# New hand-planned step orders for all five engines of an attention kernel

## The chip, the cores and the metric

The kernel runs on one core of one Trainium2 chip. A core has TensorE (PE) for matmuls, VectorE (DVE), ScalarE (ACT) and GpSimd (POOL) for elementwise work, and SyncE (SP), whose queue here issues every DMA. The metric is the device time in microseconds (us) of one execution; the median of several runs is compared.

## The reference

A layer of conditioned attention with a residual, over 8 batches of 512 rows and 1024 columns, 16 heads of 64, all in float32:

```
scale, shift = split(cond @ W_emb + b_emb)
xn  = rms_norm(x, g_norm) * (1 + scale) + shift
q, k, v = heads(xn @ W_qkv);  q, k = rms_norm(q, g_q), rms_norm(k, g_k)
o   = softmax(q k^T / 8) v                 # per head
out = x + o + o @ W_out
```

## The kernel before

Every float32 operand of a matmul is split into a high and a low part (names ending in `_hi`, `_lo`; `q_split` and `v_split` hold both), and a product is made of two or three matmuls. For every split ACT makes the high part and DVE or POOL subtracts it to get the low part.

Work comes in batches (8) and pairs of heads (8 in a batch, so 4 couples of two pairs). The projection to q, k, v of a couple of pairs uses seven products in place of eight, on sums of blocks of xn and of the weights. The weights are split once, in batch 0: loaded raw into `w_raw` and its like, summed (DVE takes even blocks, POOL odd ones), split into a ring `w_ring` of 15 chunks, and stored to `qkv_store` and `wo_store`. Later batches reload them from there, each unit as soon as the ring's space is free. So batch 0 has much more DVE, ACT, POOL and DMA work than the others. Before it comes a short stage that computes scale and shift.

The order of work on each engine is written out by hand, as a table of steps in three versions: `HEAD` for batch 0, `BODY` for batches 1 to 6, `TAIL` for batch 7. A step is a pair number, a letter and a number: `0C8` is step 8 of kind C for pair 0, in BODY pairs 8 to 11 are the next batch's 0 to 3, and a + in place of the pair means work for the next batch. The same letter on two engines means two parts of the same thing. Each engine runs its list strictly in order, and steps wait for each other through semaphores. The letters used below:

- PE: `C` a part of a tile of the projection (six matmuls, lines 597 to 599), `P` the same of the output projection, `T` turning q and k, `S` scores, `F` turning probabilities into `flip_bank` (two banks), `W` product with v (line 732), `X` turning x, `Z` turning scale and shift.
- ACT: `A` sum of squares of a tile of x (line 769), `X` modulation, `Y` high part `xa_hi` of an operand, `E` copy of a projection tile, `S` exponential, `F` `pt_hi`, `O` half of o, `Q` `o_hi`, `V`, `D`, `L` (high part of a weight unit).
- DVE: `G` a sum of blocks of xn (line 1007), `Y` low part `xa_lo` (line 1058), `J` a sum of weight blocks, `L` low part of the even half of a weight unit (line 908), `D` line 1089, `S` `neg_max`, `N` scaling of `probs` by the row sums (line 1075), `F` `pt_lo` (line 1079), `R` adding the residual.
- POOL: `X` low part `xa_lo` (line 1178) of half of the operands, `J` and `L` the odd halves, `A` and `D` the reciprocal roots, `M`, `V`, `Q` (`o_lo`).
- SP: `W` reload of a weight unit (line 1266), `H` store of one (line 1254), `G` raw weights (line 1241), `X` a tile of x for the next batch (line 1275), `E` a tile of x for the residual (line 1300), `O` store of output (line 1309).

An example of a step's waits, the residual load on SP in batch 0, which wants every qkv weight unit split because it lands in `w_raw`:

```
if is_first(b) and g < NFIRST:
    for done in w_lo_even, w_lo_odd:
        sp.wait_ge(done, PAIRS // 2 * COUPLE)
```

And the product with v on PE waits for `pt_lo` of the same step, since that frees its `flip_bank`: `freed(pe, "F", n, it)`.

Of the kernel before, what the change touches and what calls it, by code (L numbers as in the profile page):

```python
# [40 lines left out]
        1F7 2C21 1W6 1W7 2C22 2C23 2C24 2T0 2T1 2C25 2C26 2C27 4C0 4C1 2S0 2S1 4C2 2S2 2S3 4C3 2S4 2S5 2S6 2S7 3T0 4C4
        3T1 2F0 4C5 4C6 2F1 2W0 2F2 4C7 3S0 3S1 2F3 2W1 2W2 3S2 2F4 4C8 3S3 4C9 4C10 2W3 2W4 2F5 3S4 3S5 2F6 4C11 2F7
        2W5 2W6 2W7 3F0 3F1 3S6 3S7 3F2 3W0 3W1 4C12 4C13 4C14 3F3 4C15 4C16 4C17 3W2 3W3 4C18 3F4 3F5 4C19 4C20 3W4 3W5
        4C21 3F6 3F7 4C22 4C23 4C24 4C25 3W6 3W7 4C26 4C27 4T0 4T1 6C0 6C1 6C2 6C3 +X0 +X4 4S0 4S1 +X1 +X5 6C4 6C5 4S2
        4S3 +X2 +X3 4S4 4S5 6C6 +X6 4F0 6C7 4S6 4S7 4W0 4F1 4F2 5T0 5T1 6C8 6C9 4W1 4W2 6C10 4F3 +X7 6C11 5S0 5S1 4F4
# [25 lines left out]
        L1 8T0 L2 7O1 8T1 9D1 7Q0 9D2 8V1 L3 8S0 8S1 9D3 8S2 8S3 L4 L5 L6 8F0 8S4 8F1 8S5 L7 8F2 8S6 8S7 9T0 8F3 9T1 8F4
        8O0 8F5 9S0 9S1 8F6 8F7 9S2 9S3 9F0 9V0 9S4 9S5 9S6 9F1 10E0 10E1 9V1 9F2 9S7 8O1 10E2 10D0 9F3 9F4 9F5 10E3
        10D1 9F6 9F7 10D2 L8 10D3 11D0 L9 L10 L11 11D1 10T0 10V0 10V1 10T1 11D2 10S0 11D3 10S1 L12 L13 L14 10S2 10S3
        10S4 L15 10F0 10S5 10S6 10S7 10F1 11T0 11T1 11S0 11S1 11S2 11S3 8Q0 9O0 12E0 9O1 10F2 10F3 9Q0 12E1""".split(),
    "VectorE": """
        X0 X4 Y0 0J0 X2 0J1 0J2 Y1 Y4 G0 G1 G2 G3 X6 G4 G5 Y5 0D0 0L4 G6 0J3 0L5 0L6 Y3 Y2 0J4 G7 0L7 0D1 0E4 0E5 0J5
        0L8 0E6 0L9 0L10 0L11 0E7 0E8 0E9 0D2 Y6 0D3 0E10 0L12 0L13 1D0 0E11 1D1 2L0 2L1 0E12 0T0 0T1 0E13 0S0 0S1 2L2
        0N0 2L3 1D2 0S2 0S3 1D3 0N1 0N2 0N3 0S4 0S5 0F0 0F1 0N4 0N5 0S6 0S7 0F2 0F3 0N6 0N7 2J0 2J1 1T0 0F4 0O0 0F5 1T1
        2J2 2J3 0F6 1S0 0F7 2D0 2L4 2L5 1S1 1N0 2L6 2L7 1N1 1S2 1S3 2E4 0O1 2D1 2L8 2E5 1S4 1S5 1N2 1N3 2L9 2J4 2E6 1S6
        1S7 1F0 2E7 1F1 1N4 1N5 1N6 1N7 1F2 1F3 2E8 2J5 2L10 1F4 2D2 2E9 1F5 2L11 2D3 1F6 1F7 2E10 2L12 2L13 1O0 1O1  # L80
        2E11 3D0 3D1 4L0 4L1 2T0 2E12 2E13 2T1 3D2 3D3 2S0 2S1 4L2 4L3 2N0 2S2 2S3 2S4 2S5 2S6 2S7 4J0 2N1 4J1 4J2 2N2
        2N3 2N4 3T0 2F0 2N5 2N6 4J3 4L4 3T1 +A0 +A1 +A2 2N7 2F1 2F2 3S0 +A3 4L5 3S1 3S2 2F3 4D0 2F4 3S3 3N0 3N1 4L6 4L7
# [1310 lines left out]
```

## Time and profile before

| what | us |
|---|---|
| median of 3 runs (lowest, highest) | 2259.87 (2258.46, 2263.42) |
| span of the profiled execution | 2255.9 |
| PE, DVE, ACT, POOL busy in it | 2176.2, 1748.6, 1411.7, 931.4 |

The profiled execution's span lies 4.0 us below the median of the timed runs. In the profile a matmul's duration includes its way through the array, and matmuls overlap; the distance from one start to the next is what one costs. A bracket at a row's end gives the idle time of the engine just ahead of that instruction, and who ended it. Busy time by stretch is printed as start:end, length, then for each engine the busy time and the count of instructions in brackets, then the granted TensorE clock as a share of 2.4 GHz (0.50 is the lower level, 1.2 GHz), the share of DMA time and GB/s.

### The profile page before, as it was taken

To read this page: it belongs to the slowest core of one execution; us is meant where nothing else is said; L and a number is where in the kernel's file an instruction comes from. 1 tells how busy PE (TensorE), PEld (TensorE's weight loads), DVE (VectorE), ACT (ScalarE), POOL (GpSimd) and SP (SyncE) were. 2 spreads that over 40 slices of the span, in tenths; PEclk is the share of its full clock that TensorE was granted. 3 is DMA by queue.
4 is the path that set the end of the run, shared out by engine and by line. 5 is a ranking of instruction groups with operands and counts; after the bars stand their busy time and mean duration, and the time that the engine had idled before them with its cause. 6 is when DMAs were issued, how large, how long until landed. Compare 5 with 4: busy or idle time off the path is not lost.

```text
span 2255.9 us, 39472 instructions
## 1 busy us (share of the span) xinstructions
PE 2176.2 (96%) x13392; PEld 1992.2 (88%) x13392; DVE 1748.6 (78%) x3511; ACT 1411.7 (63%) x3077; POOL 931.4 (41%) x1241
## 2 busy tenths in 40 slices
PE   7788789999999999999999999999999999999999
PEld 3676678999999999999999999999999999999989
DVE  4799988678985699767986689857897569876786
ACT  4577766467854577546864578646775458754663
POOL 3866674235532345223541246312553325422330
PEclk9899999999999999999999999999999999999999
DMA  7655464777556765568555675566654775656842
GB/s 299 238 212 226 188 224 147 269 269 254 192 187 241 271 218 196 175 236 289 207 202 197 230 285 192 189 238 242 230 205 165 254 281 199 203 192 227 294 157 103
DMA packets 141528, 497.55 MB, mean 221 GB/s; under 512 B 14864, under 2 KB 61968, under 8 KB 140304
## 3 DMA queue, kind: packets, MB, share of 16 engines
q1 hardware_dynamic: 141328, 495.03, 61.7%
q8 instruction: 108, 1.77, 0.3%
q14 instruction: 92, 0.75, 0.1%
HBM read 425.77 MB, written 69.21 MB: 219 GB/s over the span
## 4 chain that ended last, share of the span: by engine, by line
PE 77%; DVE 11%; issue 4%; DMA 4%; ACT 3%; POOL 1%; SPq 0%; DVEq 0%; ACTq 0%
PE proj_bank L597 16%; PE proj_bank L599 16%; PE proj_bank L598 16%; PE flip_bank L721 8%; PE pv_bank L732 5%; PE pv_bank L733 5%; PE score_bank L713 4%; PE score_bank L714 4%; DMA w_ring<-qkv_store 2%; DVE neg_max L1069 2%; DVE probs L1075 2%; PE score_bank L686 2%; DVE pt_lo L1079 1%; ACT pt_hi L866 1%; ACT probs L860 1%
## 5 line engine op out<-in xcount | busy, mean ns | idle before, releaser
L597 PE MATMUL proj_bank<-w_ring,xa_hi 128*128 128x384 f32 x1792 | 626.5, 350 | 21.0 <-DVE xa_lo L1058 7.6
L599 PE MATMUL proj_bank<-w_ring,xa_lo 128*128 128x384 f32 x1792 | 606.4, 338 | 0.0
L598 PE MATMUL proj_bank<-w_ring,xa_hi 128*128 128x384 f32 x1792 | 605.7, 338 | 0.0
L860 ACT ACTIVATE probs<-score_bank,neg_max 128x512 f32<-128x512 f32 x512 | 352.1, 690 | 250.0 <-DVE neg_max L1069 242.6
L866 ACT CAST pt_hi<-flip_bank 128x512 fp32r<-128x512 f32 x512 | 296.3, 586 | 235.7 <-PE flip_bank L721 148.3
L1079 DVE TENSOR_TENSOR pt_lo<-flip_bank,pt_hi 128x512 fp32r<-128x512 f32 x512 | 346.6, 686 | 117.0 <-ACT pt_hi L866 111.6
L1069 DVE TENSOR_REDUCE neg_max<-score_bank 128x1 f32<-128x512 f32 x512 | 341.4, 684 | 75.0 <-PE score_bank L714 71.7
L597 PEld LDWEIGHTS proj_bank<-w_ring,xa_hi 128*128 128x128 f32 x1792 | 340.6, 190 | 40.8 <-issue 13.5
L598 PEld LDWEIGHTS proj_bank<-w_ring,xa_hi 128*128 128x128 f32 x1792 | 341.3, 190 | 9.6
L599 PEld LDWEIGHTS proj_bank<-w_ring,xa_lo 128*128 128x128 f32 x1792 | 339.6, 190 | 0.0
L721 PE MATMUL flip_bank<-ident,probs 128*128 128x128 f32 x2048 | 294.3, 274 | 14.5 <-DVE probs L1075 7.3
L721 PEld LDWEIGHTS flip_bank<-ident,probs 128*128 128x128 f32 x2048 | 245.9, 141 | 59.4 <-issue 12.5
L1075 DVE TENSOR_SCALAR probs<-probs,row_inv 128x512 f32<-128x512 f32 x512 | 277.9, 543 | 18.2
L597 PE MATMUL proj_bank<-w_ring,o_hi 128*128 128x256 f32 x992 | 285.4, 288 | 0.0
L599 PE MATMUL proj_bank<-w_ring,o_lo 128*128 128x256 f32 x992 | 280.3, 283 | 0.0
L598 PE MATMUL proj_bank<-w_ring,o_hi 128*128 128x256 f32 x992 | 279.8, 282 | 0.0
L1190 POOL TENSOR_TENSOR qk_rstd<-qk_ms_eps,neg_half 128x4 f32<-128x4 f32 x256 | 269.1, 1051 | 20.0
L1171 POOL TENSOR_TENSOR v_split<-stage,v_split 128x256 fp32r<-128x256 f32 x128 | 97.0, 758 | 431.1 <-ACT v_split L833 430.6
L732 PE MATMUL pv_bank<-pt_hi,v_split 128*128 128x512 f32 x512 | 219.9, 430 | 14.1 <-DVE pt_lo L1079 13.5
L713 PE MATMUL score_bank<-k_hi,q_split 128*128 128x512 f32 x512 | 214.0, 418 | 14.2 <-ACT probs L860 8.3
L1187 POOL TENSOR_TENSOR qk_ms_eps<-qk_ms,eps_col 128x4 f32<-128x4 f32 x256 | 62.0, 242 | 393.7 <-DVE qk_ms L1089 393.6
L967 DVE TENSOR_TENSOR stage<-proj_bank,stage 128x384 f32<-128x384 f32 x256 | 141.2, 555 | 105.2 <-PE proj_bank L599 101.4
(91 smaller groups left out, 3855.3 us busy)
## 6 DMA issues: line engine op xcount, KB each, us to landing
w_ring<-qkv_store SPq DMA_DIRECT2D x392, 768.0 KB, 5.7
w_ring<-wo_store SPq DMA_DIRECT2D x108, 512.0 KB, 4.7
qkv_store<-w_ring SPq DMA_DIRECT2D x56, 768.0 KB, 4.9
x_tile<-in_x SPq DMA_DIRECT2D x36, 512.0 KB, 7.8
w_raw<-in_x SPq DMA_DIRECT2D x112, 128.0 KB, 6.4
out<-w_raw SPq DMA_DIRECT2D x112, 128.0 KB, 1.9
w_raw<-in_w_qkv SPq DMA_DIRECT2D x16, 768.0 KB, 7.8
wo_store<-w_ring SPq DMA_DIRECT2D x16, 512.0 KB, 5.0
```

The lines of the kernel that those rows point to most:

```text
L597: nc.tensor.matmul(dst, a_hi, w[:, 0, :], start=start, stop=False, skip_group_check=shared)
L598: nc.tensor.matmul(dst, a_hi, w[:, 1, :], start=False, stop=False, skip_group_check=shared)
L599: return nc.tensor.matmul(dst, a_lo, w[:, 0, :], start=False, stop=stop, skip_group_check=shared)
L713: nc.tensor.matmul(score_bank[n % 2][:, :], q_t, k_hi[h][:, :], start=True, stop=False)
L721: mm = nc.tensor.transpose(flip_bank[u % 2][:, qt * P:(qt + 1) * P], probs[h][:, qt, i * P:(i + 1) * P], ident[:, :])
L732: nc.tensor.matmul(pv_bank[h][:, :], v_t, pt_hi[n % 2][:, :], start=(i == 0), stop=False)
L860: nc.scalar.activation(probs[h][:, i, :], score_bank[n % 2][:, :], ACT.Exp, bias=neg_max[:, n:n + 1], accum_out=row_sum[:, n:n + 1]).then_ ...
L866: nc.scalar.copy(pt_hi[n % 2][:, :], flip_bank[u % 2][:, :]).then_inc(flip_hi, 1)
L1069: nc.vector.tensor_reduce(neg_max[:, n:n + 1], score_bank[n % 2][:, :], AX.X, ALU.max, negate=True).then_inc(max_done, 1)
L1075: nc.vector.tensor_scalar(probs[h][:, i, :], probs[h][:, i, :], row_inv[:, n:n + 1], None, ALU.mult).then_inc(probs_ready, 1)
L1079: nc.vector.tensor_tensor(pt_lo[n % 2][:, :], flip_bank[u % 2][:, :], f32(pt_hi[n % 2][:, :]), ALU.subtract).then_inc(flip_freed["VectorE" ...
L1190: nc.gpsimd.tensor_tensor(qk_rstd[:, n, :], qk_ms_eps[:, n, :], neg_half[:, :], ALU.pow).then_inc(qk_rstd_done, 1)
```

## The change

Only the three tables are replaced. Each engine's list in each table holds exactly the same steps as before, in another order; no step moves to another engine, and the code that carries them out is the same (13 lines lower, since the tables are longer). Steps shift by 1 to 3 places on average, at most 34, and on SP in BODY by 8 on average, at most 47. The new orders were planned with DVE's two-tensor operations taken as longer while POOL runs. Two lines of the 311 stand for the rest, the start of DVE's list in HEAD:

```diff
-        X0 X4 Y0 0J0 X2 0J1 0J2 Y1 Y4 G0 G1 G2 G3 X6 G4 G5 Y5 0D0 0L4 G6 0J3 0L5 0L6 Y3 Y2 0J4 G7 0L7 0D1 0E4 0E5 0J5
...
+        X0 X4 Y0 X2 0J0 Y1 0J1 Y4 G0 0L4 G1 0J2 G2 X6 G3 G4 Y5 G5 G6 Y3 G7 Y2 0L5 0L6 0J3 0E4 0L7 0D0 0E5 0L8
```

**DVE in batch 0, ahead of the operand for PE's 0C8.** The last row of each piece is `Y2`, the low part that 0C8 waits for. Before:

```order
L1058 TENSOR_TENSOR xa_lo<-x_tile1,xa_hi 128x4x128
L1089 TENSOR_REDUCE qk_ms<-sq 128x4
L908 TENSOR_TENSOR w_ring<-w_raw,w_ring 128x384
L1007 TENSOR_TENSOR x_tile2<-x_tile3,x_tile2 128x512
L926 TENSOR_TENSOR w_raw<-w_raw 128x384
L908 TENSOR_TENSOR w_ring<-w_raw,w_ring 128x384
L908 TENSOR_TENSOR w_ring<-w12_raw,w_ring 128x384
L1058 TENSOR_TENSOR xa_lo<-x_tile1,xa_hi 128x4x128
L1058 TENSOR_TENSOR xa_lo<-x_tile0,xa_hi 128x4x128
```

Now:

```order
L1071 TENSOR_TENSOR xa_lo<-x_tile1,xa_hi 128x4x128
L1020 TENSOR_TENSOR x_tile3<-x_tile2,x_tile3 128x512
L1020 TENSOR_TENSOR x_tile2<-x_tile3,x_tile2 128x512
L1071 TENSOR_TENSOR xa_lo<-x_tile1,xa_hi 128x4x128
L1020 TENSOR_TENSOR x_tile2<-x_tile2 128x512
L1071 TENSOR_TENSOR xa_lo<-x_tile0,xa_hi 128x4x128
```

`0D0`, `0J3`, `0L5` and `0L6` now stand behind `Y2`, and `G7` ahead of it; `0L4` has moved further up. On POOL the six sums of `0J0` to `0J3` now stand ahead of `X7`, its first operand, and not behind it; `1D1` and `1M0` now stand behind `X13`, its last operand of the batch, and `0V0` ahead of it.

**SP in batch 0, the first reloads for batch 1.** `w_ring<-qkv_store` is a reload (8W0 first), `w_raw<-in_x` a residual load (E0 to E3). Before:

```order
L1254 DMA qkv_store<-w_ring 128x1536 x2
L1300 DMA w_raw<-in_x 128x2x128 x4
L1266 DMA w_ring<-qkv_store 128x1536
L1254 DMA qkv_store<-w_ring 128x1536
L1266 DMA w_ring<-qkv_store 128x1536 x13
```

Now:

```order
L1267 DMA qkv_store<-w_ring 128x1536 x2
L1279 DMA w_ring<-qkv_store 128x1536
L1313 DMA w_raw<-in_x 128x2x128
L1267 DMA qkv_store<-w_ring 128x1536
L1279 DMA w_ring<-qkv_store 128x1536 x3
```

The reload 8W0 now stands ahead of all residual loads, and only one of these stands ahead of 8W1. DVE's `6L13`, the split that E0 waits for, stands ahead of `6E9`, `5F6`, `5F7`, `6D2` and `6D3`, which were ahead of it.

**SP at the start of each of batches 1 to 6.** `x_tile<-in_x` are the four tiles of x for the next batch (the `+X` steps), behind the last store of the batch before. Before:

```order
L1309 DMA out<-w_raw 128x2x128
L1300 DMA w_raw<-in_x 128x256
L1275 DMA x_tile<-in_x 128x1024 x4
L1300 DMA w_raw<-in_x 128x256 x11
L1266 DMA w_ring<-qkv_store 128x1536 x38
```

Now:

```order
L1322 DMA out<-w_raw 128x2x128
L1288 DMA x_tile<-in_x 128x1024
L1279 DMA w_ring<-qkv_store 128x1536
L1313 DMA w_raw<-in_x 128x256 x3
L1288 DMA x_tile<-in_x 128x1024
L1279 DMA w_ring<-qkv_store 128x1536 x3
L1288 DMA x_tile<-in_x 128x1024 x2
```

The first tile is now issued one DMA sooner, the other three later and one by one, and the twelve residual loads are spread over the batch. In the same place PE's order changes from `4C4 2F4 2W2 2F5 2W3 4C5 2W4` to `4C4 4C5 2W2 2F4 2W3 2F5 4C6 2F6 2W4`, ACT's from `+A0 2F4 3V0 2F5 2F6` to `+A0 2F4 2F5 4E2 3V0 2F6`, and POOL's from `0Q0 1Q0 3V0 +A0` to `0Q0 +A0 1Q0 3V0`.

## Rows read from the trace of the kernel before

**Rows 1.** The page: span, and busy time of two engines.
```profile
span 2255.9 us, 39472 instructions
...
PE 2176.2 (96%) x13392; PEld 1992.2 (88%) x13392; DVE 1748.6 (78%) x3511; ACT 1411.7 (63%) x3077; POOL 931.4 (41%) x1241
```

**Rows 2.** Busy time of each engine by stretch, whole run.
```profile
37.00:70.00 33.00, 18.70 (x102) 16.63 (x102) 30.04 (x50) 19.88 (x47) 20.90 (x16) 0.80 0.42 171
70.00:100.00 30.00, 25.99 (x128) 25.02 (x127) 17.04 (x29) 14.33 (x32) 27.55 (x32) 0.84 0.80 303
100.00:345.00 245.00, 205.54 (x1080) 174.86 (x1079) 223.22 (x413) 178.31 (x398) 160.34 (x182) 0.95 0.53 204
345.00:490.00 145.00, 143.43 (x951) 134.86 (x950) 112.26 (x231) 82.74 (x191) 51.66 (x75) 1.00 0.67 228
490.00:2083.00 1593.00, 1584.31 (x9985) 1478.55 (x9985) 1232.52 (x2524) 1014.01 (x2196) 614.53 (x853) 1.00 0.63 222
2083.00:2256.00 173.00, 168.16 (x1093) 156.32 (x1091) 125.43 (x256) 91.46 (x197) 46.87 (x66) 1.00 0.52 188
```

**Rows 3.** What PE waited for in 37 to 490: total, times, longest.
```profile
PE proj_bank L597 <- DVE xa_lo L1058: 7.6, 1, 7.6
...
PE proj_bank L597 <- DMA w_ring<-qkv_store: 3.6, 2, 2.3
```

**Rows 4.** PE in order of time, the first couple of batch 0.
```profile
68.39 0.66 PE L597 MATMUL proj_bank<-w_ring,xa_hi 128*128 128x384 f32 x1 [7.63 <-DVE xa_lo L1058]
...
95.10 0.66 PE L597 MATMUL proj_bank<-w_ring,xa_hi 128*128 128x384 f32 x1 [3.53 <-POOL xa_lo L1178]
```

**Rows 5.** The same columns as group 2, just behind that first wait.
```profile
68.00:73.00 5.00, 4.61 (x14) 4.64 (x15) 2.55 (x6) 1.14 (x2) 2.39 (x3) 0.50 0.29 118
```

**Rows 6.** DVE in order of time, 42 to 69.
```profile
42.53 0.68 DVE L1058 TENSOR_TENSOR xa_lo<-x_tile,xa_hi 128x512 fp32r<-128x512 f32 x1
...
49.40 2.91 DVE L1058 TENSOR_TENSOR xa_lo<-x_tile,xa_hi 128x512 fp32r<-128x512 f32 x2
...
61.60 0.41 DVE L1089 TENSOR_REDUCE qk_ms<-sq 128x4 f32<-128x256 f32 x1
...
63.47 0.55 DVE L926 TENSOR_TENSOR w_raw<-w_raw 128x384 f32<-128x384 f32 x1
63.94 1.01 DVE L908 TENSOR_TENSOR w_ring<-w_raw,w_ring 128x384 fp32r<-128x384 f32 x2
64.88 3.41 DVE L1058 TENSOR_TENSOR xa_lo<-x_tile,xa_hi 128x512 fp32r<-128x512 f32 x2
```

**Rows 7.** POOL in order of time, 44 to 95.
```profile
44.28 1.26 POOL L1178 TENSOR_TENSOR xa_lo<-x_tile,xa_hi 128x512 fp32r<-128x512 f32 x1 [8.10 <-ACT xa_hi L817]
...
93.69 1.26 POOL L1178 TENSOR_TENSOR xa_lo<-x_tile,xa_hi 128x512 fp32r<-128x512 f32 x1
```

**Rows 8.** The DMA queue (SPq), then PE, around 307 to 320.
```profile
307.23 2.02 SPq L1300 DMA_DIRECT2D w_raw<-in_x  x4
309.36 0.40 SPq L1266 DMA_DIRECT2D w_ring<-qkv_store  x1
...
319.31 0.65 PE L597 MATMUL proj_bank<-w_ring,xa_hi 128*128 128x384 f32 x1 [2.32 <-DMA w_ring<-qkv_store]
```

**Rows 9.** Start of batch 3: the DMA queue, ACT, PE.
```profile
1021.57 2.17 SPq L1275 DMA_DIRECT2D x_tile<-in_x  x4
...
1028.67 1.06 ACT L769 ACTIVATE square_out<-x_tile 128x1024 bf16<-128x1024 f32 x1 [1.89 <-DMA x_tile<-in_x]
...
1031.16 0.47 PE L732 MATMUL pv_bank<-pt_hi,v_split 128*128 128x512 f32 x1 [1.04 <-DVE pt_lo L1079]
```

**Rows 10.** What PE waited for in 2083 to 2256.
```profile
PE pv_bank L732 <- DVE pt_lo L1079: 1.2, 1, 1.2
```

**Rows 11.** The probs scaling on DVE, 100 to 345, then 345 to 2256.
```profile
L1075 DVE TENSOR_SCALAR probs<-probs,row_inv 128x512 f32<-128x512 f32 x56 | 40.3, 719 | 2.0
...
L1075 DVE TENSOR_SCALAR probs<-probs,row_inv 128x512 f32<-128x512 f32 x456 | 237.7, 521 | 16.2
```

More of the change, by code:

```diff
@@ L41 @@
[L41 to L45, printed above, removed]
@@ new lines @@
+    "GpSimd": """
+        0J0 0J1 0J2 0J3 X7 0L4 X11 X8 X12 X10 0L5 X9 0L6 0L7 0J4 0L8 0D0 0L9 0J5 0L10 0M0 0L11 0L12 0D1 0M1 0D2
+        0D3 0M2 0M3 0V0 0L13 1D0 X13 2L0 2L1 1D1 1M0 2L2 2J0 1D2 1D3 0V1 1M1 1M2 2J1 1M3 2L3 1V0 2J2 2J3 2L4 2L5
+        1V1 2L6 2L7 2J4 2L8 2D0 2L9 2D1 2M0 0Q0 2L10 2J5 2D2 2L11 2L12 2M1 2M2 2V0 2D3 2M3 2L13 4L0 3D0 4L1 3D1
+        3M0 2V1 3M1 4L2 3D2 3D3 3M2 4J0 4J1 3M3 +A0 +A1 1Q0 4L3 +A2 +A3 4J2 4L4 4J3 4L5 3V0 4L6 4J4 3V1 4L7 4J5
+        4L8 4D0 4L9 4L10 4L11 2Q0 4M0 4D1 4D2 4L12 4L13 4D3 4M1 4M2 6L0 4V0 6L1 6L2 5D0 4M3 6J0 5M0 6J1 5D1 6L3
+        6J2 6J3 5M1 6L4 4V1 5D2 5D3 5M2 +X7 5M3 6L5 +X8 6D0 6L6 6L7 6L8 6J4 6L9 5V0 3Q0 6J5 5V1 6L10 6M0 +X1 6D1
+        6M1 +X0 6L11 6L12 4Q0 +X4 6L13 +X3 6D2 6D3 6M2 6M3 +X11 7D0 +X5 7D1 +X12 6V0 7D2 +X10 7M0 6V1 +X9 7M1
+        7M2 7D3 7M3 +X13 +X6 +X2 8D0 7V0 5Q0 7V1 8D1 8M0 8M1 6Q0 L0 8D2 8D3 8M2 8M3 L1 L2 8V0 L3 7Q0 9D0 9D1 8V1
+        L4 9D2 9M0 L5 9M1 L6 9D3 9M2 9M3 L7 9V0 9V1 10D0 10M0 10D1 10D2 10M1 10M2 10D3 L8 10M3 L9 L10 L11 L12
+        11D0 11D1 11M0 11M1 L13 11D2 11M2 11D3 L14 11M3 L15 10V0 10V1""".split(),
@@ L159 @@
-    "GpSimd": """
-        0Q0 1Q0 3V0 +A0 3V1 4D0 2Q0 4D1 +A1 +A2 +A3 4M0 4M1 4D2 4M2 4D3 4V0 4M3 3Q0 4V1 5D0 5M0 5D1 5D2 5D3 5M1 5M2 5M3
-        +X0 6D0 +X7 +X1 5V0 +X8 5V1 6M0 6D1 4Q0 6M1 +X4 +X11 6D2 6D3 6M2 6M3 7D0 +X5 +X10 +X3 +X9 6V0 7M0 7D1 6V1 7D2
-        +X12 7D3 7M1 7M2 7M3 8D0 +X2 5Q0 8M0 7V0 7V1 +X6 +X13 8D1 8D2 8M1 8M2 8D3 8M3 6Q0 7Q0 9D0 9M0 8V0 9D1 9M1 9D2
-        9M2 9D3 9M3 8V1 9V0 9V1 10D0 10D1 10M0 10M1 10D2 10D3 10M2 10M3 11D0 11D1 10V0 11D2 11M0 11M1 11D3 11M2 11M3
-        10V1""".split(),
@@ new lines @@
+    "GpSimd": """
+        0Q0 +A0 1Q0 3V0 3V1 +A1 4D0 2Q0 +A2 4D1 4D2 +A3 4M0 4M1 4M2 4D3 4M3 5D0 4V0 4V1 3Q0 5D1 5M0 5M1 5D2 +X0
+        5M2 5D3 5M3 6D0 +X7 +X1 +X8 6M0 5V0 5V1 6D1 4Q0 6M1 +X4 +X11 6D2 6D3 6M2 6M3 7D0 6V0 +X5 7M0 +X10 +X3
+        +X9 7D1 7M1 6V1 +X12 7D2 7D3 7M2 7M3 +X2 7V0 8D0 5Q0 7V1 8M0 6Q0 8D1 8D2 8M1 8M2 8D3 +X6 8M3 +X13 9D0
+        9M0 7Q0 9D1 9D2 8V0 9M1 8V1 9M2 9D3 9M3 9V0 9V1 10D0 10M0 10D1 10M1 10D2 10M2 10D3 10M3 11D0 11D1 11M0
+        10V0 11D2 11D3 11M1 11M2 11M3 10V1""".split(),
@@ L204 @@
-        6W12 6W13 W0 W1 W2 W4 W5 W6 W8 W9 W10 W12 W13 W14 W3 W7 W11 W15 O0 O1 O2 O3 O4 O5 O6 O7 O8 O9 O10 O11 O12 O13
-        O14 O15""".split(),
+        E0 4W4 4W5 4W6 4W7 4W8 4W9 4W10 4W11 E1 E2 4W12 E3 4W13 6W0 6W1 6W2 6W3 6W4 6W5 6W6 6W7 6W8 6W9 6W10
+        6W11 6W12 6W13 W0 W1 -O15 W2 W4 W5 W6 W8 W9 W10 W12 W13 W14 W3 W7 W11 O0 O1 O2 O3 O4 W15 O5 O6 O7 O8 O9
+        O10 O11 O12 O13 O14 O15""".split(),
 }
```

279 lines of the change are left out of this document (143 added, 136 removed).

## The prediction

> **What bounds the kernel now.** I read the page first: PE is busy for 2176.2 of 2255.9 us, 96% [rows 1]. So all that a new order can win is idle time of PE, some 80 us, and time that PE spends at its lower clock. Next I split the span at the batches. From 490 to 2083, batches 1 to 6, PE is busy for 1584.31 of 1593 us: 8.7 us are idle, 1.4 us a batch. Batch 7 and the end idle for 173 - 168.16 = 4.8 us. From 37 to 490, batch 0, the idle times are 14.3, 4.0, 39.5 and 1.6 us, together 59.4, and the granted clock is 0.80, 0.84 and 0.95 in the first three stretches where it is 1.00 later [rows 2]. So most of what can be won lies in batch 0, ahead of 345. What stands beside PE there is DVE: 30.04 of 33 us and 223.22 of 245 us busy, but only 17.04 of 30 us from 70 to 100 [rows 2]. DVE paces batch 0, and in 70 to 100 it has room because PE was late.
>
> The list of what PE waited for names single events. PE waits 7.63 us at 0C8 for `xa_lo` from DVE, and 3.53 us at 0C26 for `xa_lo` from POOL [rows 3, 4]. It waits 3.6 us, in two waits, for reloaded weights of batch 1, the second of 2.32 us ending at 319.31 [rows 3, 8]. Right behind the first wait the granted clock is 0.50, the lower of the two levels, for the next 5 us [rows 5], so a long wait costs more than its length.
>
> **Part 1, the operand for 0C8.** Ahead of it DVE is hardly idle (30.04 of 33 us busy up to 70, [rows 2]), so 0C8 comes when DVE has done what stands ahead of `Y2`, whose pair of instructions ends at 64.88 + 3.41 = 68.29, just ahead of PE's 68.39 [rows 4, 6]. The change takes `0D0` (0.41), `0J3` (0.55) and `0L5`, `0L6` (1.01) from ahead of it and puts `G7` there, a two-tensor operation on 128x512 for which I take the 0.68 of an `xa_lo` that runs alone: 1.97 - 0.68 = 1.3 us won [rows 6]. Second, the overlap with POOL. An `xa_lo` takes 0.68 us at 42.53, while POOL is idle, and 1.46 each at 49.40 and 1.71 each at 64.88, while POOL is at work [rows 6, 7]. POOL is idle for 8.10 us up to 44.28, and the six sums of `0J0` to `0J3` now stand ahead of `X7` and fall into this gap [rows 7]. Behind `X7` POOL must then wait for ACT's part of `0L4`, and DVE works alone for a while. If that frees one pair from its stretch, it is 2.91 - 1.36 = 1.55 us; the bounds are 0 and both pairs, 1.55 + 2.05 = 3.6. I take 1.7. Against it, `Z` now stands behind a second `X` on PE, so DVE starts its modulation later, and POOL's `0L5` stands behind `X12` and `X10`, which wait for ACT; 0C9 needs it. No row shows these two. I take 0.5 for both. Sum: 1.3 + 1.7 - 0.5 = 2.5 us, with 0 and 5 as bounds. The wait stays some 5 us long, so I give nothing for the clock here.
>
> The scaling of `probs`, with a single tensor input, is slowed as well: it means 719 ns between 100 and 345, where POOL is busy for 160.34 of 245 us, and 521 behind that [rows 2, 11]. That is 56 x 0.2 = 11 us of DVE in batch 0 which a plan that stretches two-tensor operations alone does not see, and it is the ground of case B below. The Trainium skill has a rule on this in "SBUF — State Buffer", section "SBUF: two separate sides": VectorE and GpSimd share one pair of ports as an exclusive lock, the loser blocks for the other's whole instruction, and it holds for VectorE's modes with two ports as for two SBUF inputs. By the rule alone the 11 us would stay whatever the new plan does, and DVE would pace batch 0 as before: the sum would be that of B, 2255. By the rows DVE has idle time to work with, and the sum is the one below.
>
> **Part 2, the operand for 0C26.** POOL is busy for 27.55 of 30 us from 70 to 100, and its `X13` starts at 93.69, ahead of PE's start at 95.10 [rows 2, 4, 7]. Six sums are now done in the idle time ahead of 44.28, and `1D1` and `1M0` go behind `X13` while `0V0` comes ahead. An `xa_lo` of 512 elements takes POOL 1.26 us [rows 7], so a sum of 384 some 0.95 and the six 5.7. If two thirds of that are kept until `X13`, the wait of 3.53 us is gone. A half clock for 5 us, as behind the first wait [rows 5], loses 2.5; I give 1 us for a clock that does not fall here. 0 to 4.5, I take 4.5.
>
> **Part 3, the first reloads.** SP is one queue in order. At 307.23 it issues E0 to E3, which had waited for DVE's last split `6L13`; 8W0 follows at 309.36, 8W1 behind one more store, and PE's 8C1 can only start at 319.31 [rows 8]. Now 8W0 stands ahead of E0, and 8W1 behind E0 and one store. Three residual loads of 2.02 / 4 = 0.5 us each and one reload of 0.4 leave the path of 8W1 [rows 8], and `6L13` stands ahead of one eviction, two `pt_lo` and two `D`. Taken as 0.55, 2 x 0.68 and 2 x 0.41, as for instructions of their size in [rows 6], that is 2.7 us sooner. Together 1.9 + 2.7 = 4.6 us, more than the 3.6 us of waits, so these go. DVE follows PE here, so what is won is kept only as far as DVE has idle time: 245 - 223.22 = 21.8 us from 100 to 345 [rows 2]. 0 to 5, I take 4.
>
> **Batch 0 together** is 2.5 + 4.5 + 4 = 11 us. But DVE has the same instructions as before, and paces this batch. It could do it: it was idle for 3 + 13 + 21.8 us of the 308 [rows 2]. I take off 3 us for waits that come up at other places: 8 us.
>
> **Part 4, the start of batches 1 to 6.** In batch 3 SP issues the four x tiles from 1021.57; ACT's `+A0`, first in its list, waits 1.89 us for the first and starts at 1028.67, 7.1 us behind the issue; F4 is stuck behind `+A0` on ACT, and PE's 2W4 waits 1.04 us for `pt_lo` [rows 9]. Now X0 is issued one DMA sooner, about 0.5 us (2.17 / 4), and PE has `4C5` ahead of `2F4`, so that 2F4 and 2W4 come later on PE by a C or so. A C step is six matmuls, and 951 of them took 143.43 us [rows 2]: 0.9 us. Together 1.4 us exceed the wait of 1.04. On SP, X1 to X3 now stand behind the reload 4W4, which waits for ring space; what hides it is that ACT takes `+A1` only some 15 steps later, and if it doesn't, ACT stands still there as it does now for X0. All six batches idle for 8.7 us on PE [rows 2]; I take it that this start and smaller waits make up half of what is curable: 4 us of 8.7, with 0 and 8 as bounds.
>
> **Part 5, the end.** Batch 7 has one wait of 1.2 us for `pt_lo` [rows 10], behind a run of DVE work from which the change takes two `D` (2 x 0.41). I take 1 us.
>
> **The sum.** 8 + 4 + 1 = 13 us off a span of 2255.9: 2243. The median lies 4.0 us above the profiled span, so 2247.
>
> **The rivals.** A difference of less than 0.2% (4.5 us) can't be told from none here.
>
> A, as summed, 2238 to 2254. For it: the three events of batch 0 are single, long, and each is reached by the change. Chance 0.57.
>
> B, DVE takes back what batch 0 won. PE comes sooner to the pairs' softmax, and DVE, with the same work and scalings that the plan did not stretch, is late by as much there. Only parts 4 and 5 stay, at most half of part 3: 5 to 7 us won at best, 3 at worst, 2253 to 2257. For it: DVE at 91% in 37 to 70 and 100 to 345. Against it: 13 us of idle DVE in 70 to 100 [rows 2]. Chance 0.16, half of it faster by the bound.
>
> C, no change: the new order has as many small waits as the old, since six batches idle for only 1.4 us each and there the order can mostly lose. 2256 to 2264. Chance 0.12.
>
> D, slower: the wait at the start of a batch grows. `+A0` on ACT and POOL's `+A0`, now ahead of `1Q0` (`o_lo` of pair 1), both hang on the landing of X0. ACT's `2O0` needs that `o_lo`, and behind it stand `4E3` and the next `pt_hi`, for which PE waits. X0 landed 7.1 us behind its issue [rows 9]; the room beyond that no row gives, I choose 2 us. Each us beyond it costs six. It would lose part 4 too, so that it cancels the other 9 us from 1.5 us beyond the room, and a landing 3 us beyond it, 12 us behind the issue, gives 2260 - 9 + 18 = 2269. Against it: fewer DMAs are issued right behind X0 than before. With other losses of its sign, 0.15.
>
> The range that leaves out no more than 2 in 10 runs from 2236 to 2264; A's own is 2238 to 2254. Faster: 0.57 + 0.08 + 0.03 = 0.68. Same 0.17, slower 0.15.
>
> **What would show it.** In the new profile the first wait of `proj_bank` for `xa_lo` from DVE is about 5 us and the wait for POOL's `xa_lo` is gone; PE is busy for more than 27 of the 30 us from 70 to 100; no wait for `w_ring<-qkv_store` near 8C1; batch 1 starts 8 us sooner than 490; and six batches take some 1589 us. I am wrong if batch 1 starts no sooner though the three waits are gone (B), or if PE's idle time in batches 1 to 6 is over 12 us (D).

## The result, and the profile after

The changed kernel takes 2224.0 us (median, 2221.83 to 2227.42), the kernel before 2260.48 in the same comparison: ratio 0.984, 95% interval 0.9826 to 0.9854. It is 36 us faster; forecast were 13, and the time lies below the range. The page of the profiled run, and its stretches (span and engines as in [rows 1, 2]):

```profile
span 2220.0 us, 39472 instructions
...
PE 2161.7 (97%) x13392; PEld 1985.8 (89%) x13392; DVE 1727.3 (78%) x3511; ACT 1415.2 (64%) x3077; POOL 911.8 (41%) x1241
```
```profile
36.00:70.00 34.00, 23.36 (x119) 20.85 (x118) 30.09 (x50) 20.97 (x49) 21.55 (x18) 0.80 0.42 172
70.00:100.00 30.00, 25.68 (x143) 24.05 (x142) 23.78 (x45) 18.21 (x41) 28.07 (x34) 1.00 0.95 361
100.00:345.00 245.00, 217.70 (x1208) 190.18 (x1207) 227.07 (x447) 189.88 (x422) 160.61 (x196) 0.98 0.56 213
345.00:461.00 116.00, 115.48 (x789) 109.50 (x788) 83.66 (x179) 66.67 (x154) 39.51 (x59) 1.00 0.70 244
461.00:2047.00 1586.00, 1581.90 (x9987) 1479.09 (x9986) 1230.08 (x2525) 1016.49 (x2197) 606.95 (x853) 1.00 0.64 223
2047.00:2220.00 173.00, 168.43 (x1093) 156.22 (x1091) 125.30 (x259) 92.45 (x197) 45.74 (x66) 1.00 0.54 191
```

Batch 1 starts 28.6 us sooner, batches 1 to 6 take 1586 us where they took 1593, batch 7 and the end the same 173. For PE the two things that the prediction looked at, its idle time and its clock, both moved. DVE works for 18 us less in batch 0 with nearly the same instructions (697 and 699 in the rows further down), and the scaling of `probs` shows it; where [rows 11] had 719 ns between 100 and 345, there is now:

```profile
L1088 DVE TENSOR_SCALAR probs<-probs,row_inv 128x512 f32<-128x512 f32 x61 | 34.2, 561 | 2.2
```

PE in order of time at 0C8 and 0C26 (as [rows 4]), and the stretch behind the first wait (as [rows 5]):

```profile
64.02 0.66 PE L610 MATMUL proj_bank<-w_ring,xa_hi 128*128 128x384 f32 x1 [3.99 <-ACT stage L808]
...
90.64 0.41 PE L610 MATMUL proj_bank<-w_ring,xa_hi 128*128 128x384 f32 x1 [1.52 <-POOL xa_lo L1191]
```
```profile
64.00:69.00 5.00, 4.98 (x16) 5.00 (x17) 4.79 (x5) 0.24 (x1) 5.00 (x5) 0.50 0.50 205
```

In the tables below, batch 0 is cut at PE's steps 0C0, 0C27, 4C0, 5S4, 8C0 and 7S0 and at the 4C0 of batch 1. Ahead of each of them both orders have the same set of steps on PE, so a stretch holds the same work in both. The places were found by counting PE's matmuls through the order list.

```
stretch from, us         0C0    0C27   4C0    5S4    8C0    7S0     together
before                   50.7   66.7   119.8  32.0   29.9   144.3   443.4
changed                  45.6   59.6   111.8  31.3   23.4   143.5   415.0
won                       5.2    7.1     8.1   0.7    6.5     0.8    28.3
```

The last column as rows of before and of the changed kernel (columns of [rows 2]):

```profile
46.43:489.81 443.38, 387.87 (x2214) 346.70 (x2213) 375.38 (x699) 290.01 (x652) 258.11 (x303) 0.95 0.58 213
```
```profile
46.21:461.25 415.04, 376.32 (x2215) 340.08 (x2213) 357.48 (x697) 290.50 (x653) 243.33 (x297) 0.98 0.61 225
```

One trace can't tell small differences: two other traces in which batch 0 has the orders of before gave 446 and 449 in place of 443.4, and two with the changed orders 414 and 419 in place of 415.0, so less than some 5 us of it needs the timed runs.

### The profile page after: what moved, and what is told of

Read it like the earlier page. It is cut to its first block, busy times and chain, and to the rows that moved or that the text cites. A ratio compares the mean times of both kernels' runs of the same rounds, so it can differ in the third digit from the quotient of the medians.

```text
span 2220.0 us, 39472 instructions
## 1 busy us (share of the span) xinstructions
PE 2161.7 (97%) x13392; PEld 1985.8 (89%) x13392; DVE 1727.3 (78%) x3511; ACT 1415.2 (64%) x3077; POOL 911.8 (41%) x1241
## 4 chain that ended last, share of the span: by engine, by line
PE 86%; DVE 4%; ACT 3%; DMA 3%; issue 2%; POOL 1%; SPq 0%; ACTq 0%; DVEq 0%; POOLq 0%
PE proj_bank L610 18%; PE proj_bank L612 17%; PE proj_bank L611 17%; PE flip_bank L734 9%; PE score_bank L726 5%; PE score_bank L727 5%; PE pv_bank L745 5%; PE pv_bank L746 5%; PE score_bank L699 2%; DMA w_ring<-qkv_store 2%; PE flip_bank L706 1%; ACT k_hi L858 1%; PE proj_bank L757 1%; PE score_bank L757 1%; DMA w_raw<-in_x 1%
## 5 line engine op out<-in xcount | busy, mean ns | idle before, releaser
L1092 DVE TENSOR_TENSOR pt_lo<-flip_bank,pt_hi 128x512 fp32r<-128x512 f32 x512 | 346.7, 685 | 106.2 <-ACT pt_hi L879 101.6
L1088 DVE TENSOR_SCALAR probs<-probs,row_inv 128x512 f32<-128x512 f32 x512 | 263.9, 516 | 18.2
L1203 POOL TENSOR_TENSOR qk_rstd<-qk_ms_eps,neg_half 128x4 f32<-128x4 f32 x256 | 262.1, 1024 | 20.1
L727 PE MATMUL score_bank<-k_lo,q_split 128*128 128x512 f32 x512 | 203.6, 398 | 0.0
```

The costliest lines, as they stand in the source:

```text
L727: nc.tensor.matmul(score_bank[n % 2][:, :], q_t, k_lo[h][:, :], start=False, stop=True).then_inc(score_full, 1)
L1088: nc.vector.tensor_scalar(probs[h][:, i, :], probs[h][:, i, :], row_inv[:, n:n + 1], None, ALU.mult).then_inc(probs_ready, 1)
L1092: nc.vector.tensor_tensor(pt_lo[n % 2][:, :], flip_bank[u % 2][:, :], f32(pt_hi[n % 2][:, :]), ALU.subtract).then_inc(flip_freed["VectorE" ...
```

## The experiments

### Where in batch 0 the gain arises

Four kernels have the changed orders up to a place and those of before behind it (last step of the changed part):

```
             PE     ACT    DVE    POOL   SP
front_only   0C27   0T1    0D2    0M3    before
to_4C0       2C27   3D3    3D3    3M1    before
to_6C11      6C12   +Y4    5F4    +X2    before
head_only    all of batch 0 on all five; batches 1 to 7 of before
```

> The orders of the changed kernel on PE, ACT, DVE and POOL as far as 0C27, and behind it those of before (SP's order is that of before). It holds parts 1 and 2 of the prediction and nothing else. Theory S (the gain is DVE time: the scaling of probs is stretched less by POOL, all along batch 0): at 0C27 PE is 4.5 to 6 us earlier and this is kept, so batch 1 starts 4 to 7 us earlier and the time is 4 to 7 us below before, 0.997 to 0.998. Theory W (single waits, as the prediction summed them): 7 us at 0C27, kept, 7 us in all. Theory B (DVE takes it back): PE is as early at 0C27, but batch 1 starts within 2 us of before.

Measured: 0.9992 (0.9978 to 1.0005), 1.8 us. PE is 4.3 us earlier at 0C27, 4.1 at 5S4 and 2.3 at batch 1. The interval ends at 5.0 us: W's 7 us lie outside, S's 4 to 7 only touch it, and B's figure is the nearest. PE in order of time, and what PE waited for in 310 to 335:

```profile
63.86 0.66 PE L600 MATMUL proj_bank<-w_ring,xa_hi 128*128 128x384 f32 x1 [4.00 <-ACT stage L798]
90.80 0.66 PE L600 MATMUL proj_bank<-w_ring,xa_hi 128*128 128x384 f32 x1 [3.52 <-POOL xa_lo L1181]
```
```profile
PE proj_bank L600 <- DMA w_ring<-qkv_store: 4.4, 2, 2.3
```

The first wait is halved, but the second is as long as it was (3.53). POOL's `X13` did come 4.3 us sooner, and so did PE. Of what is left, some goes at the reloads, whose wait grew from 3.6 to 4.4.

> The same, but the changed orders go on to 2C27, just ahead of 4C0. Theory S: 12 us at 4C0 as in the changed kernel, kept to batch 1, so 11 to 13 us in all, and the scaling of probs takes less DVE time ahead of 164 alone. Theory W: nothing is added to the run before it, since no long single wait of before lies between 0C27 and 4C0; 7 us. Theory B: within 3 us of before.

Measured: 0.9977 (0.9965 to 0.9988), 5.2 us. PE is 9.0 us earlier at 4C0 and 3.2 at batch 1: the stretch from 4C0 to 5S4, in the order of before, now took 122.9 and not 119.8. S had forecast 11 to 13 us and is too high; W's 7 us lie within the interval (2.7 to 7.9), B's 3 at its edge.

> The same, but the changed orders go on to 6C11, about 260 us into the span, ahead of the first reloads. Theory S: 20 us at 6C12, of which 18 to 21 arrive at batch 1, since the waits for the reloads behind it are part of SP's order and can grow by what PE comes earlier, up to 3 us. Theory W: 7 us at most. Theory B: within 3 us of before at batch 1.

Measured: 0.9912 (0.9888 to 0.9936), 19.9 us; 19.1 at 5S4, 17.2 at batch 1. The stretch from 4C0 to 5S4 took 111.6 us. W, with 7 us at most, is refuted: no long wait of [rows 3] lies between 0C27 and 5S4, and yet more than half of batch 0's gain arises there.

> All five engines in the changed orders in the program's first part (batch 0), the orders of before in batches 1 to 7. Every theory expects batch 1 to start 28 us earlier, as in the changed kernel. Batches 1 to 6 then take as long as before or up to 1.2 us each less if the gain there came from the state in which batch 0 leaves the engines. Time: before minus 28, so 2232 (0.988), if the 7 us of batches 1 to 6 come from their own order; 2225 if not.

Measured: 0.9879 (0.9857 to 0.9901), 27.3 us; 24.6 at batch 1. The other 8 us are the order of batches 1 to 7.

> The orders of before, with those of the changed kernel only between 2C27 and 6C11 on PE and at the corresponding places on ACT, DVE and POOL (about 160 to 270 us); SP's order is that of before. The run that had this stretch and what is ahead of it won 19 us, the one without the stretch 5. If the stretch stands for itself: 12 to 15 us. If it needs what the front won: under 8 us. At 6C12 PE is then 8 to 11 us earlier.

Measured: 0.9963 (0.9951 to 0.9975), 8.4 us, of the 15 that `to_6C11` has over `to_4C0`. The stretch took 112.0 us, as in the changed kernel; 8.7 us at 5S4 and 5.7 at batch 1. So the stretch wins its 8 us by itself, under the 12 to 15 of the first expectation; what `to_6C11` has beyond that came only together with the front.

### SP's order of the reloads

`sp_only` and `sp_back` exchange SP's list in batch 0 (its core below; the `+X` loads, too, stand further up in the new one).

```diff
-... 6H11 6H12 E0 E1 E2 E3 8W0 6H13 8W1 8W2 8W3
+... 6H11 6H12 8W0 E0 6H13 8W1 8W2 8W3 E1
```

> The kernel before with SP's new order in batch 0 alone: 8W0 and 8W1 ahead of the first output stores and residual loads. PE, ACT, DVE and POOL in the orders of before. Part 3 of the prediction: the two waits for w_ring (3.6 us) shrink by the 1.9 us that leave SP's queue, and what is won is 1.5 to 3.6 us. Theory S: as DVE paces the batch, 0 to 2 us of it arrive at batch 1. Theory that the reload order is the largest single part: 5 us, as much as the gain grew at 8C1 in the changed kernel (from 21 to 26 us).

> The changed kernel with SP's old order in batch 0 alone. By part 3, PE then waits for the reloads again at 8C0 and 8C1; PE comes there 21 us earlier, and the reloads hang on DVE's 6L13 and the DMAs before them, so the wait is 3 to 8 us, and 3 to 5 us of it stay in the time (2227 to 2229). Theory S allows the same or less, 0 to 5. If the time is unchanged, SP's order was worth nothing.

Measured: `sp_only` 0.9972 (0.9961 to 0.9983), 6.3 us; in its trace PE has no wait for `w_ring<-qkv_store` between 285 and 330. `sp_back` 2231.54 us, 0.9877 (0.9858 to 0.9895), which is 7.5 above the changed kernel. In its trace, PE at 8C0 and 8C1:

```profile
296.51 0.41 PE L609 MATMUL proj_bank<-w_ring,xa_hi 128*128 128x384 f32 x1 [0.77 <-DMA w_ring<-qkv_store]
...
300.15 0.44 PE L609 MATMUL proj_bank<-w_ring,xa_hi 128*128 128x384 f32 x1 [2.36 <-DMA w_ring<-qkv_store]
```

The two waits are 3.1 us together, but SP's order is worth 6 to 8 us, so not all of it hangs on them. Against the changed kernel PE in this trace is 2.1 us later at 8C0, 2.9 more at 7S0 and 5.4 more at batch 1. Behind 7S0 it waits four times for reloads of later units, where the changed kernel waits once, 0.5 us, and the kernel before not at all:

```profile
PE proj_bank L609 <- DMA w_ring<-qkv_store: 3.4, 4, 2.1
```

The reading that SP's order is the largest of the parts that the prediction named holds, but it is the whole order of SP in batch 0 and not only 8W0 and 8W1.

### DVE's own time

```diff
+                        part = slice(0, T // 2) if it < PAIRS else slice(0, T)
-                        nc.vector.tensor_scalar(probs[h][:, i, :], probs[h][:, i, :], row_inv[:, n:n + 1], None,
+                        nc.vector.tensor_scalar(probs[h][:, i, part], probs[h][:, i, part], row_inv[:, n:n + 1],
```

> The kernel before, but in batch 0 the scaling of probs works on 256 of the 512 columns, so it leaves out half of that computation in batch 0. The orders are those of before. It takes 0.13 us less each, 91 times, and less of it is stretched: DVE has 12 to 18 us less to do. Theory S (DVE time sets the length of batch 0): batch 1 starts 10 to 18 us earlier though every order and every wait rule is that of before. Theory W (only single waits count): batch 1 starts no more than 3 us earlier, and 0C8 and 0C26 wait as before.

Measured: 0.9975 (0.9963 to 0.9987), 5.6 us; in the trace 2.4 at batch 1. The edit reached 64 scalings, those of the eight pairs of batch 0, and not the 91 of the window, and took 7.8 us off DVE (367.58 us) and not 12 to 18. The time lies between what S and W forecast; this run alone decides nothing.

```diff
+                        if it < PAIRS:
+                            nc.vector.reciprocal(spare[:, n:n + 1], row_sum[:, n:n + 1])
                         nc.vector.reciprocal(row_inv[:, n:n + 1], row_sum[:, n:n + 1]).then_inc(inv_done, 1)
```

> The changed kernel with one more reciprocal of 0.15 us ahead of each scaling of probs in batch 0, into a spare column: 96 in all, 14.8 us more on DVE. The orders are those of the changed kernel. Theory S: batch 1 starts 10 to 15 us later and the time is 2234 to 2239. Theory W: under 3 us later, as DVE is idle for 26 us of the batch. Between: the part of each added microsecond of DVE that arrives at the end of batch 0, which prices the 11.6 us that the scaling lost to POOL less in the changed kernel.

Measured: 2223.41 us, 0.9845 (0.9823 to 0.9867); nothing lost, as W forecast and S did not. But the dose was too small to tell: again 64 and not 96, and each takes less of DVE than its duration, since instructions overlap in the records. The next pair has three of them. 

> The kernel before with three more reciprocals of 0.15 us into spare columns ahead of each of the 64 scalings of probs of batch 0's eight pairs: 192 x 0.155 = 30 us more of plain DVE work, which POOL does not hold up. DVE was idle for 36 us of the batch. If DVE's time sets the batch's length, 20 to 30 us of them arrive at batch 1. If not, under 10.

> The changed kernel with the same 30 us. One reciprocal per scaling, 10 us, had cost nothing there. DVE is idle for 26 us of the batch. If that idle time was a reserve that the smaller dose just used up: 10 to 20 us later at batch 1. If DVE's time sets the length and the smaller dose was lost in noise: 20 to 30. If only places matter: under 8.

Measured: before_dose 1.0032 (1.0021 to 1.0043), 7.3 us more; after_dose 2233.02 us, 0.9876 (0.9854 to 0.9898), 9.0 more than the changed kernel. DVE in order of time in before_dose:

```profile
128.08 0.28 DVE L1075 RECIPROCAL spare<-row_sum 128x1 f32<-128x1 f32 x3
128.27 0.15 DVE L1076 RECIPROCAL row_inv<-row_sum 128x1 f32<-128x1 f32 x1
```

Three start within 0.19 us, so one costs 0.06 us and not 0.155, and the 192 cost 12 us and not 30. Batch 0 from 0C0 on, before_dose, then after_dose:

```profile
45.40:498.94 453.54, 393.77 (x2214) 349.99 (x2213) 383.44 (x891) 291.24 (x652) 258.35 (x303) 0.93 0.56 207
```
```profile
48.35:475.25 426.90, 382.86 (x2214) 343.96 (x2213) 368.28 (x889) 291.42 (x653) 245.44 (x297) 0.97 0.60 219
```

DVE has 8.1 and 10.8 us more, and batch 0 is 10.2 and 11.9 us longer in these traces, 7.3 and 9.0 in the timed runs. The bounds of the expectations were set for 30 us and don't hold for this dose; measured against what DVE really got, most of the plain DVE time added to this batch arrives. The small changes, 4.3 us more in after_recip (nothing lost) and 7.8 less in before_half (5.6 won), are of the size of their intervals and add little to that.

### The hold-up by itself

How a hold-up looks, in the kernel before: DVE in order of time, then POOL.

```profile
255.89 1.05 DVE L1075 TENSOR_SCALAR probs<-probs,row_inv 128x512 f32<-128x512 f32 x1
256.87 0.15 DVE L1073 RECIPROCAL row_inv<-row_sum 128x1 f32<-128x1 f32 x1
257.05 1.03 DVE L1075 TENSOR_SCALAR probs<-probs,row_inv 128x512 f32<-128x512 f32 x1
258.00 0.15 DVE L1073 RECIPROCAL row_inv<-row_sum 128x1 f32<-128x1 f32 x1
258.19 0.49 DVE L1075 TENSOR_SCALAR probs<-probs,row_inv 128x512 f32<-128x512 f32 x1
```
```profile
255.33 2.47 POOL L1133 TENSOR_TENSOR w_ring<-w_raw,w_ring 128x384 fp32r<-128x384 f32 x2
```

The same scaling takes 0.49 us alone and 1.03 to 1.05 when it starts beside POOL's two splits. Beside a power on POOL it does not grow (DVE, then POOL):

```profile
462.69 0.49 DVE L1075 TENSOR_SCALAR probs<-probs,row_inv 128x512 f32<-128x512 f32 x1
```
```profile
462.19 1.03 POOL L1190 TENSOR_TENSOR qk_rstd<-qk_ms_eps,neg_half 128x4 f32<-128x4 f32 x1
```

What the changed order does with it can be counted in the two traces, from 0C0 to batch 1 (before, then now: the scaling and `pt_lo`):

```profile
L1075 DVE TENSOR_SCALAR probs<-probs,row_inv 128x512 f32<-128x512 f32 x91 | 59.9, 658 | 3.2
L1079 DVE TENSOR_TENSOR pt_lo<-flip_bank,pt_hi 128x512 fp32r<-128x512 f32 x82 | 54.7, 684 | 10.8 <-ACT pt_hi L866 10.0
```
```profile
L1088 DVE TENSOR_SCALAR probs<-probs,row_inv 128x512 f32<-128x512 f32 x89 | 48.3, 542 | 3.2
L1092 DVE TENSOR_TENSOR pt_lo<-flip_bank,pt_hi 128x512 fp32r<-128x512 f32 x82 | 55.6, 684 | 9.0 <-ACT pt_hi L879 8.1
```

Of the scalings 29 were longer than 0.55 us before and 11 are now (29 to 31, and 11 to 13, in other traces with these orders). POOL's wide operations (all but the powers and their sums with eps) now lie beside instructions that they don't lengthen: they overlap 60 of the 82 `pt_lo` for 34.9 us, where it was 40 for 21.6, and the mean stays 684 ns; `neg_max` goes from 23.7 to 34.7 us at 683 ns.

A first pair of kernels tried to make the scaling immune by reading its row in steps of two:

```diff
+                        if it < PAIRS:
+                            row = row.rearrange("p (n s) -> p s n", s=2)
```

> The kernel before, but the scaling of probs in batch 0's eight pairs (64 instructions) goes through its row in steps of two elements, the even ones and then the odd ones. The result is the same. If this form runs on DVE without the fast mode, each takes some 0.75 us whether or not POOL is at work, so the long ones of 0.9 to 1.5 us are gone, and DVE has 17 us more of plain work. Theory S2 (what costs is not the sum of DVE's time but single scalings that POOL holds up while PE waits for them): the time falls or stays, batch 1 starts 0 to 10 us earlier. Theory S (DVE's sum counts): batch 1 starts 6 to 12 us later. Theory O (the order of the steps itself, not the stretch): 0 to 5 us later, the price of the longer plain form.

> The changed kernel with the same stepped scaling. With before_stride it makes a table of two orders by two forms. Theory S2: the changed order has little left to win where no scaling is held up, so the gap between the two orders shrinks from 36 us to below 20. Theory O: the gap stays above 28. Theory S: both are later by the same 6 to 12 us. If the stepped form is held up by POOL just as the plain one, the profile shows it in the spread of its durations, and the pair says nothing on S2.

Measured: 0.9996 (0.9985 to 1.0008) and 0.9836 (0.9814 to 0.9858), as without the edit. The scaling still took some 490 ns alone and up to 1.49 us beside POOL, so the pair says nothing on S2. It serves as a repeat of both kernels.

The second pair leaves DVE alone and gives POOL other work of the same length:

```diff
+                first_batch[0] = b == 0
...
+                cut = dst[:, 0:n].rearrange("p (a b) -> p a b", b=b)
+                return nc.gpsimd.tensor_tensor(cut, eps_col[:, 0:b].unsqueeze(1).to_broadcast([P, a, b]),
+                                               neg_half[:, 0:b].unsqueeze(1).to_broadcast([P, a, b]), ALU.pow)
```

> The kernel before, but in batch 0 POOL's two-tensor operations (the low parts of weights, x and v, the sums of weights, the scaling of q and k) are replaced by powers of 1 to 6 columns into the same places, of about the same duration on POOL; only o_lo is still computed. So it leaves out these computations in batch 0, and four tensors are set to zero while DVE is idle at the start. The orders are those of before. In the traces so far a power on POOL never lengthened an instruction of DVE (73 scalings of probs inside one took 489 ns, as 487 alone), so DVE's instructions are no longer held up. Theory L (what was won is DVE held up less by POOL): DVE is busy 17 to 20 us less in batch 0 and batch 1 starts 15 to 25 us earlier. Theory O (the order of the steps): under 8 us earlier.

> The changed kernel with the same edit. Theory L: it has less hold-up left to lose, so batch 1 starts 5 to 10 us earlier than in the changed kernel, and the gap between the two orders at batch 1, 28 us with POOL's real work, is 15 or less without the hold-up. Theory O: the gap at batch 1 stays at 24 or more.

Measured: before_nolock 2229.31 us, 0.9857 (0.9839 to 0.9876), 30 us faster than before; after_nolock 2212.22, 0.9782 (0.9762 to 0.9803), 12 faster than the changed kernel. The gap between the orders falls from 36 us to 17. In the traces DVE is busy for 39.4 us less than before and batch 1 starts 26.8 us sooner, twice the DVE time that theory L had set (17 to 20) and a little more than its 15 to 25 at batch 1; in after_nolock batch 1 starts 7.6 us sooner, and the gap at batch 1 is 9.4. POOL's new instructions are about as long as the old ones (POOL is busy for 249.65 us of batch 0 and not 258.11); its splits took 1044 ns in before, and in before_nolock (with DVE's scaling under it, 658 ns in this window before):

```profile
L1141 POOL TENSOR_TENSOR w_ring<-eps_col,neg_half 128x4 fp32r<-128x4 f32 x68 | 71.2, 1055 | 16.1 <-ACT w_ring L761 15.9
```
```profile
L1077 DVE TENSOR_SCALAR probs<-probs,row_inv 128x512 f32<-128x512 f32 x91 | 47.0, 517 | 3.2
```

From 4C0 to 5S4, in before, the changed kernel, before_nolock and after_nolock:

```profile
163.86:283.69 119.83, 95.74 (x492) 80.95 (x492) 111.65 (x204) 88.91 (x203) 79.73 (x94) 0.93 0.54 213
```
```profile
151.34:263.10 111.76, 91.88 (x493) 78.93 (x492) 102.84 (x205) 89.41 (x204) 74.40 (x93) 0.95 0.57 225
```
```profile
153.23:259.45 106.22, 91.67 (x492) 76.91 (x493) 97.36 (x204) 88.93 (x203) 74.93 (x94) 0.97 0.61 241
```
```profile
150.33:257.69 107.36, 90.36 (x494) 77.71 (x493) 96.66 (x205) 89.54 (x204) 71.02 (x92) 0.97 0.59 235
```

DVE is busy for 92 to 93% of the time in the first two and PE for 80 to 82%: here DVE paces. The changed order needs 8.8 us less of DVE and 8.1 us less in all. Without the hold-up the two orders take the same time (106.2 and 107.4). By stretches:

```
stretch from, us         0C0    0C27   4C0    5S4    8C0    7S0     together
won, POOL as it is        5.2    7.1     8.1   0.7    6.5     0.8    28.3
won, without hold-up      3.9    0.7    -1.1   2.3    5.2     0.2    11.2
```

The whole of batch 0 in before_nolock and in after_nolock:

```profile
45.22:463.06 417.84, 381.03 (x2215) 341.56 (x2213) 335.97 (x699) 290.56 (x652) 249.65 (x303) 0.97 0.61 226
```
```profile
46.95:453.63 406.68, 374.95 (x2215) 339.56 (x2213) 332.33 (x697) 290.63 (x653) 237.74 (x297) 0.98 0.63 230
```

So 17 of the 28 us of batch 0 go away with the hold-up, nearly all between 0C27 and 5S4. Theory L holds for these and theory O does not; what is left is the front and the reloads, which don't hang on it. The edit also changes the values that PE multiplies and takes 8 us off POOL itself (6 in after_nolock); no run tells these apart from the hold-up, but DVE's own times shrink by the amounts shown.

### Batches 1 to 6

`body_only` has the changed orders in batches 1 to 6 alone.

> The orders of the changed kernel in batches 1 to 6, those of before in batch 0 and batch 7. Part 4 of the prediction: 4 us, 0 to 8. By the changed kernel's trace six batches took 7.4 us less, so 7 us: 2252 to 2254. If those 7 us hang on the state in which batch 0 leaves the engines, 0 to 3 us.

Measured: 0.9979 (0.9967 to 0.9990), 4.7 us, 2.3 to 7.5, which covers the 7 and barely the 3 of the expectation. The traces decide: batches 1 to 6 take 1585.6 us here, as in the changed kernel, and 1593.9 in head_only, where they have the orders of before. Their gain stands for itself.

## Why the prediction was right in its direction and wrong in size

**The sum.** It had 8 us for batch 0, 4 for batches 1 to 6, 1 for the end. The traces show 28.6, 7.4 and 0.0.

**The step that failed** is "Batch 0 together". It says "DVE has the same instructions as before, and paces this batch", and takes off 3 us. The pacing was right (the larger doses bear it out), the premise was not: nearly the same instructions took 375.38 us of DVE in the one order and 357.48 in the other, and 11.6 of these 17.9 us are the scaling of `probs` (59.9 and 48.3). Between 0C27 and 5S4 the sum had nothing, since no long wait of [rows 3] lies there; 15.2 us were won there, while DVE's busy time fell by 12.7 (172.45 to 159.75), and without the hold-up the two orders differ by -0.4 there. The ground for it stood in the prediction: 11 us of stretched scalings [rows 11]. They were taken as fixed, "which a plan that stretches two-tensor operations alone does not see". They were not fixed: POOL's wide operations moved from beside the scalings to beside `pt_lo` and `neg_max`. That the plan did this by keeping them clear of DVE's two-tensor operations is argued, not shown. Against before_nolock, before is held up for 39.4 us of DVE (375.38 - 335.97), where the prediction saw 11; against after_nolock, the changed kernel for 25.2. The one unstretched pair of part 1 (1.7 us) was the right mechanism, priced at one place out of many.

**Part 1**, 2.5 us with a wait of some 5 left: PE starts 0C8 4.4 us sooner after a wait of 3.99. Near the upper bound of 5, and right in kind: of the pair of `xa_lo`, 1.71 us each, one is now 0.68. But the row names ACT's copy `stage` as what ended the wait, not DVE's `xa_lo` as forecast. By the records ACT's copy ends at 63.79 and DVE's `Y2` at 63.92, so two paths now end together and DVE's alone could win little more. No credit for the clock was right at this place: it is 0.50 behind the shorter wait too.

**Part 2**, 4.5 us and the wait gone: wrong by itself. In front_only the wait is 3.52. The price took the wait of 3.53 as gone if POOL won 3.8 us, but PE comes 4.3 us sooner to it, so both would have had to be made up. In the changed kernel it is 1.52, but PE waits for POOL twice more just ahead of it (1.44 for `stage`, 0.96 for a weight unit), together 3.9 us, where it was 3.5 and 0.5. What was won there is the clock: the matmul behind the wait takes 0.41 us and not 0.66. In head_only, with the same orders in batch 0, it takes 0.66. All of parts 1 and 2, forecast 7, are 1.8 us in the time when they stand alone.

**Part 3**, 4 us: 6.3 and 7.5. The mechanism was right and the size too small: in sp_back more than half of the loss at batch 1 (5.4 of 10.4 us in the trace) arises behind 7S0, at reloads that the sum did not look at. The stretch from 8C0 to 7S0 is 6.5 us shorter, of which the granted clock is a part (0.89 in before, 1.00 after); the sum counted the waits only.

**Part 4**, 4 us of 0 to 8: 7.4 in the trace, 4.7 in the timed run alone. D did not come: PE's idle time in batches 1 to 6 is 4.1 us (1586 - 1581.90), where it was 8.7. PE's waits for `pt_lo`, 2.8 us in 7 times in batches 1 to 6 before, are gone, as the prediction had it for 2W4; so are 3.4 us for ACT's `probs`, which it had not named, and six waits for ACT's `stage`, 2.4 us together, are new.

**Part 5**, 1 us: nothing. The `pt_lo` wait of 1.2 [rows 10] is down to 0.3, but reloads are waited for in its place (batch 7 and the end in the changed kernel):

```profile
PE proj_bank L610 <- DMA w_ring<-qkv_store: 1.4, 2, 0.8
PE pv_bank L745 <- DVE pt_lo L1092: 0.3, 1, 0.3
```

**The clock.** From 0C0 to batch 1 PE is busy for 387.87 us before and 376.32 after, with the same matmuls: 11.6 of the 28.3 us are matmuls that ran faster, at a mean granted clock of 0.98 and not 0.95, and 16.8 are idle time. The sum had 1 us for the clock. It moves with the other causes: in before_nolock, with the order of before and fewer waits, PE is busy for 381.03.

**The signs.** The first wait is 4.0 us and not about 5, ended by ACT and not by DVE, and the wait for POOL's `xa_lo` is shorter and not gone. PE is busy for 25.68 of 30 us from 70 to 100 and not for over 27: that sign failed though PE got through more (143 matmuls and not 128), because each ran faster at a granted clock of 1.00 and not 0.84. The reload wait is gone, batch 1 starts 28.6 us sooner instead of 8, six batches take 1586 and not 1589. Rival B is refuted: the stretch of the scalings did not stay. What failed is the step to it: that scalings which are held up in the one order are held up as often in another. They were 29 and are 11.

**Open.** Most of the added DVE time arrives, but of the hold-up removed from before only 25.5 of 39.4 us do, and of that removed from the changed kernel 8.4 of 25.2. PE alone needs some 375 us of the batch, so there is less and less to win; this is a reading, and which waits take over was not traced. Nor is it shown which moves of the order avoid the hold-up.

## What to carry to other kernels

Where an engine paces a stretch, its busy time need not be a constant of its instruction list: compare the mean duration of one instruction alone and beside the other engine, and price a reordering by how much of that difference it can take away, over the whole stretch. A list of long waits finds events and is blind to a stretch that is slow evenly. Two waits in a row on one engine are not worth their sum, as what the first gives back brings PE sooner to the second.

## What was not expected of the hardware

A scaling of 128x512 on DVE (SBUF to SBUF, one tensor) takes 0.49 us alone. Of the 66 in the whole trace of before that start while a wide two-tensor operation of POOL runs, the mean is 0.87 and the longest 1.48; DVE's weight splits go from 674 ns on average to 521 in before_nolock, its `xa_lo` from 1334 to 684. A power of some 1.03 us on POOL holds up none of them: the scalings of that trace that lay wholly inside one, another 66, took 487 ns on average and 491 at most. The Trainium skill, "SBUF — State Buffer", section "SBUF: two separate sides", says that whoever starts first has the shared ports for its whole instruction. For POOL's wide operations the traces agree in kind: 0.87 us on average where POOL started first, and 0.57 for the 42 scalings that started ahead of POOL's operation. For the powers, taken as long as the profile shows them, they don't, and the measurement decides.

Steps of two elements in its operands left the scaling at 0.49 us (median 490 ns in before_stride), with the same hold-up (up to 1.49 us).
